# Layer 1 of a four-layer megakernel: the top-k searches of a pair of attention heads shared out one to three instead of two to two

## The reference, cut to what matters

```python
# attention of layer 1, per head
q = rotary(xn @ wq); k = rotary(xn @ wk); v = xn @ wv
s = where(valid, (q @ k.T) * scale, neg)        # window of 128 keys
out = softmax(s) @ v
x += concat(out over 16 heads) @ wo
# routing of layer 1
aff = sigmoid(flat_x @ gate_w + expert_bias)            # 1024 x 7
_, topk_idx = top_k(aff, 2)
mask = (topk_idx[:, :, None] == arange(7)).any(axis=1)
score = where(mask, aff, -1.0).T                        # 7 x 1024
_, sel_idx = top_k(score, 146)                          # capacity = 1024 // 7
inp = flat_x[sel_idx]                                   # routed tokens
```

## Time and profile before

| | us |
|---|---|
| median of three runs | 713.36 |
| the profiled execution | 716.17 |
| its span | 714.6 |
| TensorE matmul busy | 656.6 (92%) |
| VectorE busy | 522.6 (73%) |
| ScalarE busy | 349.5 (49%) |
| GpSimd busy | 321.0 (45%) |

### The profile page before, as it was taken

The page is one execution under the profiler, slowest core; times in us unless marked ns, Lnnn a source line. Parts: engine busy times, 40 slices in busy tenths (PEclk is TensorE's granted clock), DMA queues, the critical chain, the costliest instruction groups (busy, mean ns, idle before and its releaser), DMA issues. The chain is left out here.

```text
span 714.6 us, 13386 instructions
## 1 busy us (share of the span) xinstructions
PE 656.6 (92%) x4794; PEld 491.2 (69%) x4794; DVE 522.6 (73%) x1068; ACT 349.5 (49%) x751; POOL 321.0 (45%) x255
## 2 busy tenths in 40 slices
PE   3999999999799999999999999989978989877987
PEld 1445555588477987878798887869867648545566
DVE  4287676593699889797979987566356888489694
ACT  1575111210455574756556575644455661496641
POOL 1000988400357676474758666897167332300100
PEclk9999999999999999999999999999999999999999
DMA  8701000000601001010101001114121100100001
GB/s 259 312 2 60 1 1 2 1 0 1 227 17 39 23 7 37 22 37 15 37 22 35 23 9 48 47 36 145 43 70 45 31 0 1 38 0 0 2 1 59
DMA packets 14646, 31.34 MB, mean 44 GB/s; under 512 B 1838, under 2 KB 8588, under 8 KB 14030
## 3 DMA queue, kind: packets, MB, share of 16 engines
q1 hardware_dynamic: 12813, 26.46, 11.1%
q0 software_dynamic: 1536, 3.15, 1.6%
q10 hardware_dynamic: 256, 1.18, 0.6%
HBM read 26.59 MB, written 5.24 MB: 45 GB/s over the span
## 5 line engine op out<-in xcount | busy, mean ns | idle before, releaser
L585 PE MATMUL bank<-zone 128*128 128x256 f32 (+1 forms) x408 | 139.8, 343 | 16.2 <-DVE arena L1661 8.5
L586 PE MATMUL bank<-zone 128*128 128x256 f32 (+1 forms) x408 | 131.4, 322 | 0.0
L587 PE MATMUL bank<-zone 128*128 128x256 f32 (+1 forms) x408 | 131.4, 322 | 0.0
L2083 POOL TENSOR_TENSOR arena<-arena 128x512 f32<-128x512 f32 x64 | 82.1, 1283 | 62.7 <-ACT arena L1260 62.7
L585 PEld LDWEIGHTS bank<-zone 128*128 128x128 f32 x408 | 77.0, 189 | 36.9 <-DVE arena L1661 13.9
L2088 POOL TENSOR_TENSOR arena<-arena 128x512 f32<-128x512 f32 x64 | 83.2, 1300 | 28.3 <-DVE arena L1661 19.1
L587 PEld LDWEIGHTS bank<-zone 128*128 128x128 f32 x408 | 77.0, 189 | 6.3
L1279 ACT ACTIVATE arena<-arena 128x256 f32<-128x256 f32 (+1 forms) x128 | 62.1, 487 | 38.4 <-DVE arena L1670 32.7
L586 PEld LDWEIGHTS bank<-zone 128*128 128x128 f32 x408 | 77.2, 189 | 3.5
L566 PE MATMUL bank<-xT,arena 128*128 128x512 f32 x160 | 77.0, 620 | 2.0 <-DMA arena<-in_lA 0.8
L1670 DVE CUSTOM_DVE_ANT_0 arena<-bank,const 128x256 f32<-128x256 f32 (+1 forms) x128 | 45.6, 402 | 28.6 <-PE bank L772 24.2
(11 more groups left out here) (289 smaller groups left out, 1362.5 us busy)
## 6 DMA issues: line engine op xcount, KB each, us to landing
arena<-in_qk SPq DMA_DIRECT2D x16, 256.0 KB
arena<-in_tern SPq DMA_DIRECT2D x1, 3072.0 KB, 22.6
arena<-in_wv SPq DMA_DIRECT2D x8, 256.0 KB, 3.0
arena<-in_wo SPq DMA_DIRECT2D x16, 128.0 KB, 2.1
arena<-in_wr SPq DMA_DIRECT2D x1, 1792.0 KB, 10.0
lB<-in_lB SPq DMA_DIRECT2D x1, 1288.5 KB, 25.1
x<-in_x SPq DMA_DIRECT2D x2, 512.0 KB, 8.2
xg_rows<-arena SPq DMA_DIRECT2D x1, 1024.0 KB
```

The costliest lines, as they stand in the source:

```text
L585: pe.matmul(dst, lhi, rhi, start=(n == 0), stop=False)
L586: pe.matmul(dst, lhi, rlo, start=False, stop=False)
L587: last = pe.matmul(dst, llo, rhi, start=False, stop=(n == len(terms) - 1 and not open_end))
L2083: pool.tensor_tensor(qraw[:, j, :], qraw[:, j, :], cosT[:, at], ALU.mult).then_inc(cos_done, 1)
```

## The change

`take_eight` is cut in two: `find_eight` (MAX8) and `strike_eight` (MATCH_REPLACE8). `head` takes four places for routing work instead of two: the two of before, a third ahead of `add_head(h, 3)`, and a fourth at the end of the head. VectorE's loop runs over four pairs, heads 0 to 7. The even head has one search (first place). The odd head has three: at the first place, at the second, and one cut in two, found at the third place and struck at the fourth. Head 8 stands behind the loop and has two as before. The other engines' programs are the same.

```diff
-            def take_eight(r):
-
+            def find_eight(r):
                 dve.wait_ge(topk, r * 2 + NB)
                 hold()
                 dve.max(top8, sT[:, 0:T]).then_inc(topk, 1)
+
+            def strike_eight(r):
                 dve.wait_ge(topk, r * 2 + (NB + 1))
                 hold()
                 dve.match_replace(sT[:, 0:T], top8, sT[:, 0:T], TAKEN).then_inc(topk, 1)
+
+            def take_eight(r):
+                find_eight(r)
+                strike_eight(r)
...
-                if choose:
-                    choose[1]()
+                choose[1]()
                 dve.wait_ge(rinv_ready, h + 1)
                 for p in range(4):
+                    if p == 3:
+                        choose[2]()
                     if last:
...
+                choose[3]()
...
-            with dve.Fori(0, ROUNDS // 2) as h:
-                head(h, choose=(lambda: take_eight(h * 2), lambda: take_eight(h * 2 + 1)))
-            head(ROUNDS // 2, choose=(last_few, weigh_tokens))
+            with dve.Fori(0, ROUNDS // 4) as i:
+                head(i * 2, choose=(lambda: take_eight(i * 4), nothing, nothing, nothing))
+                head(i * 2 + 1, choose=(lambda: take_eight(i * 4 + 1), lambda: take_eight(i * 4 + 2),
+                                        lambda: find_eight(i * 4 + 3), lambda: strike_eight(i * 4 + 3)))
+            head(ROUNDS // 2 - 1, choose=(lambda: take_eight(ROUNDS - 2), lambda: take_eight(ROUNDS - 1), nothing, nothing))
+            head(ROUNDS // 2, choose=(last_few, weigh_tokens, nothing, nothing))
```

More of the change, by code:

```diff
@@ L53 @@
 assert LEAD < CAP <= 2 * LEAD and SLOTS < T and 2 * CAP <= BW and ROUNDS // 2 + 1 < SPLIT - 2
-assert ROUNDS % 2 == 0 and REST and ROUNDS // 2 < H1
+assert ROUNDS % 4 == 2 and REST and ROUNDS // 2 < H1
 PAD = -4.0
@@ L1733, in add_rows, with nothing, head @@
                         dve.wait_ge(combined, 2 * t + 1)
-            def head(h, more=True, choose=(), base=HEAD0, last=False, beside=lambda: None):
+            def nothing():
+                pass
+            def head(h, more=True, choose=(nothing,) * 4, base=HEAD0, last=False, beside=nothing):
                 for g in (2, 3):
@@ L1742, in head @@
                         beside()
-                if choose:
-                    choose[0]()
+                choose[0]()
                 if more:
```

## The result

The changed kernel takes 707.94 us, the median of five runs (705.54 to 708.51), against 713.36 for the kernel before (five runs by then, 711.35 to 714.88): ratio 0.9925, 95% interval 0.9899 to 0.9951, so 3.5 to 7.2 us faster. The forecast was 708.8 for the median and 711.6 for the profiled execution. Timed again on another occasion (ten runs against seventeen) the ratio was 0.9931, interval 0.9908 to 0.9955, medians 707.67 and 712.21. The profiled execution took 707.98 us with a span of 706.4.

A forecast was written before the change was run, and what follows sets the result against it. TensorE bounds the kernel, waiting for VectorE's late `rotate` at odd heads' starts. Four odd heads x 1.14 = 4.6 us: profiled 716.17 to 711.6, less 2.81 to the median, 708.8 us; range for 8 in 10 706.8 to 712.0.

The forecast's parts named there:

- the lateness that goes (1.18): Start of the odd head: from transposes to projection TensorE takes 2.71 us against 1.53 in unhindered head 11; 1.18 us lost.
- the 0.04 us that the second `rotate` costs: Odd head, second projection: `rotate` number 1 was to become late next, costing 0.04 us and leaving a gain of 1.14.
- The end of the odd head: The added find and strike, 2.56 us, were to fit VectorE's waits of 1.25 and 1.29 us there; cost zero.
- The cover of 0.74 us: Behind the odd head's end: VectorE's idle time before `rotate`, waiting for ScalarE; only lateness beyond 0.74 us reaches TensorE.
- the two figures for the find: Odd head's end: the find is followed after 1.13 us, or 1.35 us where the next instruction needs its result.
- The loop: VectorE's loop body grows from 62 to 121 instructions, with four branches; cost taken as zero, between 0 and 2.48 us.
- GpSimd beside the adds: Even head: adds now run beside GpSimd's weight remainder; by the rule no contention, a small risk and no term.
- The clock: From 475 to 479 us, behind a wait for GpSimd: the clock's fall may stay or not; zero, 1.5 us either side.
- The first: Rival, heads 1, 3, 5, 7: a new wait of 0.72 us at the next projection; gain 1.8 us, 711.5; chance 0.12.
- The second: Rival, odd head's start: ScalarE's exponentials or GpSimd's chain holds it just behind VectorE; nothing moves, 713.4 us; chance 0.05.
- The third: Rival, branch behind heads 2, 4, 6, 8's strike: longer loop reloads instructions; 7.0 us lost against 4.6 gained, 715.8; chance 0.07.
- The fourth: Rival, more than forecast: the half clock stays away or the relief reaches GpSimd's chain too; 707.0 us; chance 0.08.

## Why the prediction was right

*The bound and the place.* Right. The pair with two searches in each head is slow by what TensorE loses at the start of the odd head. When only the searches move, the head follows: the odd head takes 22.34 to 22.35 us with one search in the even head before it and 23.46 with two, and with three the pair takes about 44 us.

*The size of the gain.* 1.14 us was forecast for an odd head, 1.11 came in head 3, and 4.51 / 4 = 1.13 for a pair. Of the parts, the lateness that goes (1.18) and the 0.04 us that the second `rotate` costs are both as worked out. What made the sum come out is that starts were compared with an unhindered head. The idle time alone, 0.76 us before the projection and 0.11 within the transposes, would have given 0.87.

*The even head gains nothing.* Right, 17.31 us before and 17.29 after.

*The end of the odd head.* Right: zero, by the run without the four searches. The cover of 0.74 us was also of the size that was stated, by the run with one find more. Which of the two figures for the find is right, 1.13 or 1.35 us, the changed kernel does not show: the add comes 1.34 us behind it, but it comes at that time without the find too, when TensorE delivers. With an add behind it that has nothing to wait for, the find was followed after 1.14 us (one more find in the even head).

*The loop.* Right: zero, by the run that has the loop and not the move. No instruction packet moved in it. With the rule that the prediction took from the Trainium skill's page "Advanced Engine Details and Errata", section "ISA Cache", two lines of 256 instructions, the trace agrees in so far as a body of 121 instructions brought no packet between 241 and 370 us; no run here had a body large enough to test it. The size of a line is not settled: the one packet at the loop's end has 8192 bytes in the trace, half of the 16 KB that the section gives for a line. With lines of half the size a body of 121 would still lie within two.

*GpSimd beside the adds.* GpSimd was busy 14.66 us in the even head, 14.70 before. Its two instructions beside the adds, from 263.79 us, take 2.54 us, and 2.55 in the kernel before, where they stood beside the second search. The adds do not slow it.

*The clock.* Its fall moved with the wait for GpSimd in the profiled execution (the mean from 468 to 479 us is 0.84 in both profiles), so zero was right there, and in part by luck: the same wait of 2.1 us was followed by no fall in four other executions of kernels with the same code behind the loop (below), and head 12 is 1.5 us shorter in them. That is the 1.5 us to either side that the prediction allowed.

*The rivals.* The first rested on 0.91 us of lateness in head 11, which the second profile of the kernel before does not have. A row of one execution had been read as the kernel's. The second was not met: the odd head's start moved with VectorE alone. The third was not met either, and its price, the 2.48 us of the earlier trace rows, was again a row of one execution (1.29 us in the repeat). The fourth is not met in the heads; the medians, 707.94 and 707.67, lie between its 707.0 and the forecast and do not decide.

*From the sum to the median.* 4.6 us forecast, 5.4 between the medians the first time, 4.5 the second time, 4.5 in the heads. The interval, 3.5 to 7.2, holds them all; the 0.9 us above the heads' sum are not shown to be anything but spread. The profiled execution was forecast at 711.6 us and took 707.98. The sum is not to blame: the prediction took the profiled execution of the kernel before, 2.81 us over its median and the longest of all its executions on record, as a base that would carry over. The forecast of the median does not need that step.

## What to carry to other kernels

When an engine with room over the whole span makes another one wait, lay its work beside the stretches of the chain in turn: here VectorE had under 1 us free in the even head and over four in the odd one, and moving one search of the four in a pair was worth nearly all of the wait. But room is not a sum. For each place ask which wait of the moving engine comes next and who is queued behind it; the same work in the same head was free behind one instruction and cost over 2 us ahead of another. Price a stall by comparing the starts of the same instructions in an unhindered repetition, not by the recorded wait alone, and take an odd row of one profile for the kernel's only when a second profile has it. Ask also what stands behind the piece that is moved: a search cost 2.56 us ahead of work that does not need it and 2.78 ahead of another search.

## What the runs showed of the hardware

A wait of TensorE can be paid twice. Behind waits of 0.8 to 2.5 us the granted clock often fell to the lower level, where matmuls of 128x512 start 0.43 us apart instead of 0.23. It fell at all four waits of 2.45 us, at two of four of 2.00, at eight of thirteen of about 2.1 (the one for GpSimd in head 12, one in each trace), and in two of eleven traces behind a wait of about 0.8 us in head 10, which then took 20.56 and 21.54 us instead of 19.48. What decides it is not shown. Of two executions with a wait of 2.15 and 2.14 us for GpSimd at about 469 us (the change, and the run with a find in the even head), the first has the fall and the second has not, as the stretch from 468 to 479 us shows, the change first:

```profile
468.00:479.00 11.00, 9.96 (x70) 7.34 (x71) 4.78 (x15) 5.27 (x16) 9.84 (x9) 0.84 0.15 41
```

```profile
468.00:479.00 11.00, 9.23 (x73) 7.20 (x74) 6.28 (x17) 5.47 (x16) 9.84 (x10) 1.00 0.15 41
```

Head 12 took 20.75 us in the one and 19.24 in the other, 1.5 us for the fall. The traces of kernels whose pair takes 39.65 us show four such falls in the change, its repeat and the run without the four searches (spans of 706.4, 707.5 and 707.3 us), two in the run with the third search whole at the second place (703.9) and one in the run with a find in the even head (702.5), not counting one in the last 4 us of each span. So falls of the clock account for most of what these spans differ by, while the heads repeat to 0.03 us. Where TensorE would have stood anyway, as in the run with three searches in the even head, a fall costs less.
